# A Mamba and feed-forward layer in float32 on one core: the order of the slots and the shape of the broadcast copies are changed

## The reference

```
x = layernorm(x + mamba(x))
x = layernorm(x + ffn(x))

mamba: x, z   = split(x @ in_proj.T)                    # 512 channels each
       u      = silu(conv4(x) + conv_b)                 # causal, 4 taps, per channel
       dt, B, C = split(u @ x_proj.T)                   # 64, 16, 16
       delta  = softplus(dt @ dt_proj.T + dt_b)         # 512 channels
       h[d,n] = exp(delta[d] * A[d,n]) * h[d,n] + delta[d] * u[d] * B[n]    # over time, 16 states n
       y[d]   = sum_n h[d,n] * C[n] + u[d] * D[d]
       out    = (y * silu(z)) @ out_proj.T
ffn:   silu(x @ w1.T * s1) * (x @ w2.T * s2), two hidden layers of 1024 with gelu, and w3 (256)
```

## Time and profile before

| what | value |
|---|---|
| median of three runs | 3355.04 us |
| the profiled execution | 3354.35 us, of it 3352.5 us from the first to the last instruction |
| mean granted TensorE clock | 0.884 of full speed |
| VectorE busy | 2347.6 us (70%) |
| TensorE matmuls busy | 2793.5 us (83%) |
| ScalarE busy | 2024.4 us (60%) |
| GpSimd busy | 1744.5 us (52%), all in the Mamba stage |
| moved by DMA | 404.11 MB, in 236430 packets |

### The profile page before, as it was taken

The page is one execution under the profiler, slowest core; times in us unless marked ns, Lnnn a source line. Parts: engine busy times, 40 slices in busy tenths (PEclk is TensorE's granted clock), DMA queues, the critical chain, the costliest instruction groups (busy, mean ns, idle before and its releaser), DMA issues. The chain is left out here.

```text
span 3352.5 us, 40081 instructions
## 1 busy us (share of the span) xinstructions
PE 2793.5 (83%) x10946; PEld 1629.1 (49%) x10946; DVE 2347.6 (70%) x2829; ACT 2024.4 (60%) x3344; POOL 1744.5 (52%) x892
## 2 busy tenths in 40 slices
PE   5787887887887878877878875659999999999997
PEld 2232332333333333333323332327888888888886
DVE  1988988989889889888888889444444544444443
ACT  4666666676676676676676666345555555555542
POOL 0878988888888888889788888500000000000000
PEclk8788888878888879888888887769999999999999
DMA  4454545455464554645545454372322221222210
GB/s 138 90 170 126 140 150 145 129 159 130 137 173 105 158 148 120 173 129 135 164 131 139 144 146 125 108 254 93 95 68 88 71 92 63 88 75 88 69 57 14
DMA packets 236430, 404.11 MB, mean 121 GB/s; under 512 B 23120, under 2 KB 61776, under 8 KB 236240
## 3 DMA queue, kind: packets, MB, share of 16 engines
q1 hardware_dynamic: 173328, 292.95, 31.6%
q10 hardware_dynamic: 62912, 109.08, 10.1%
HBM read 278.21 MB, written 123.73 MB: 120 GB/s over the span
## 5 line engine op out<-in xcount | busy, mean ns | idle before, releaser
L964 DVE TENSOR_TENSOR_SCAN h<-bank,state,db 128x512 f32<-128x512 f32 x1024 | 1253.7, 1265 | 64.7 <-ACT bank L700 32.7
L839 POOL TENSOR_TENSOR hc<-h,c_rows 128x1024 f32<-128x1024 f32 x512 | 1199.6, 2370 | 188.6 <-PE bank L482 182.1
L700 ACT ACTIVATE bank<-d_bc,a_neg 128x512 f32<-128x512 f32 x1024 | 694.5, 686 | 427.6 <-DVE h L964 350.2
L1191 PE MATMUL s_bank<-s_end,weights_r 128*128 128x512 f32 x2048 | 472.4, 392 | 23.7 <-DVE s_end L1284 23.7
L948 DVE TENSOR_TENSOR db<-bank,du_bc 128x2048 f32<-128x2048 f32 x192 | 435.6, 2269 | 58.9 <-DMA du_bc<-du_rows 58.8
L1251 ACT ACTIVATE s_h<-s_bank,s_sc 128x512 f32<-128x512 f32 x256 | 176.0, 688 | 486.2 <-PE s_bank L1191 485.9
L1191 PE MATMUL s_bank<-s_mid,weights_r 128*128 128x512 f32 x2048 | 466.8, 389 | 0.0
L1191 PEld LDWEIGHTS s_bank<-s_end,weights_r 128*128 128x128 f32 x2048 | 385.8, 189 | 105.6 <-DVE s_end L1284 26.2
L1191 PEld LDWEIGHTS s_bank<-s_mid,weights_r 128*128 128x128 f32 x2048 | 384.4, 188 | 79.8
L547 PE MATMUL bank<-x_t,w 128*128 128x512 f32 x1088 | 385.1, 486 | 36.2 <-ACT ab L760 29.4
L461 PE MATMUL bank<-bc,w_spread 64*128 64x512 f32 x272 | 152.1, 572 | 279.5 <-DVE db L948 204.4
(11 more groups left out here) (111 smaller groups left out, 3109.5 us busy)
## 6 DMA issues: line engine op xcount, KB each, us to landing
ab<-ab ACTq DMA_DIRECT2D x272, 256.0 KB, 4.0
d_bc<-d_rows SPq DMA_DIRECT2D x256, 256.0 KB, 5.2
du_bc<-du_rows SPq DMA_DIRECT2D x256, 256.0 KB, 8.0
s_abr<-ab SPq DMA_DIRECT2D x128, 512.0 KB, 3.9
w<-w ACTq DMA_DIRECT2D x136, 256.0 KB, 3.7
d_rows<-sp_r SPq DMA_DIRECT2D x64, 256.0 KB, 2.0
du_rows<-sp_w SPq DMA_DIRECT2D x64, 256.0 KB, 2.4
xT_sb<-in_xT SPq DMA_DIRECT2D x16, 512.0 KB, 11.6
```

Source lines behind the costliest of these rows:

```text
L700: act.activation(decays[DECAY_BANK[g]][:], d_bc[c % 2][:, j, :], ACT.Exp, scale=a_neg[:, g:g + 1]).then_inc(decay, 1)
L839: pool.tensor_tensor(hc[:, k % HCSTEPS, at:at + HG], h[:, H_SLOT[k], at:at + HG], c_rows[:, q, :].unsqueeze(1).broadcast_to([P, HG, NT]), ...
L964: dve.tensor_tensor_scan(h[:, H_SLOT[k], j, :], decays[DECAY_BANK[g]][:], db[:, k % DBSTEPS, j, :], state[:, g:g + 1], ALU.mult, ALU.add). ...
L1191: last = pe.matmul(p_h[m % HBANKS][:], weights[:, at:at + P], ins[j][:, k, :], start=k == 0 and j == 0, stop=k == KH - 1 and j == parts - 1)
```

## The change

The change has four parts.

- Slots: the 16 convolution products go into slots 0 to 10 instead of 0 to 15, SiLU of u from slot 17 to 12, x_proj from 18 to 14, the step sizes of quarter 0 from 24 to 20, SiLU of z from 40 to 63, the layer norm's last activations from 11 to 15, the transposes for `ab` from 13 and 17 to 16 and 18, and the `ab` products to a slightly different list, with the waits that go with it.
- TensorE's fold comes right at the start of a slot.
- The store to `x1` stands behind the copies of quarter 3 of the next turn. `x1` has a place for one tile more, which takes the store that the first turn makes with nothing in it. There are 17 stores instead of 16.
- The four copies of a set: before, copy nn fills the 32 partitions of state nn, all four blocks j. Now, copy j fills block j on all 128 partitions, from 32 rows of DRAM that are read four times.

```
-CONV_SLOTS = range(0, KI * TAPS)
+CONV_SLOTS = [2 * i // 3 for i in range(KI * TAPS)]
-SILU_U_SLOT = 17
-XD_SLOTS = range(18, 18 + KI)
-DT_SLOTS = (24, 38, 54, 6)
+SILU_U_SLOT = 12
+XD_SLOTS = range(14, 14 + KI)
+DT_SLOTS = (20, 38, 54, 6)
-SILU_Z_SLOT = 40
+SILU_Z_SLOT = 63
+LN_SLOT = 15
-XT_PLACES = ((13, 2), (17, 1))
-AB_PLACES = ((25, 0), (30, 2), (32, 2), (34, 2), (35, 1), (36, 2), (38, 1), (40, 1), (41, 0), (44, 2), (46, 2),
-             (48, 2), (50, 2), (52, 2), (60, 2), (62, 2))
+XT_PLACES = ((16, 2), (18, 1))
+AB_PLACES = ((23, 0), (25, 0), (28, 2), (30, 2), (32, 2), (34, 2), (36, 2), (38, 1), (40, 1), (41, 0), (44, 2), (46, 2),
+             (48, 2), (50, 2), (52, 2), (60, 2))
...
-        COPIES = 16 * GN
+        COPIES = 16 * JC
...
+            def by_state(rows, j):
+                return rows[j * GD:(j + 1) * GD, :].unsqueeze(0).broadcast_to([GN, GD, NT])
...
-                for nn in range(GN):
-                    sp.dma_start(d_bc[k][nn * GD:(nn + 1) * GD, :, :],
-                                 d_rows[k].rearrange("(j d) t -> d j t", d=GD)).then_inc(d_in[k], 16)
+                for j in range(JC):
+                    sp.dma_start(d_bc[k][:, j, :], by_state(d_rows[k], j)).then_inc(d_in[k], 16)
...
-                for nn in range(GN):
-                    sp.dma_start(du_bc[k][nn * GD:(nn + 1) * GD, :, :],
-                                 du_rows[k].rearrange("(j d) t -> d j t", d=GD)).then_inc(du_in[k], 16)
+                for j in range(JC):
+                    sp.dma_start(du_bc[k][:, j, :], by_state(du_rows[k], j)).then_inc(du_in[k], 16)
...
                 copies(t, 3)
+                store_x1(t)
...
-                sp.wait_ge(ln_out, t.count(SUB, 2 * SUB))
-                sp.sem_inc(waited, 1)
-                sp.dma_start(x1[t.b, rows, :].rearrange("(s p) c -> p s c", p=P), res[:]).then_inc(x1_out, 16)
...
+                    if n % JC == FOLD_AFTER % JC:
+                        now, g = at_group(t, n - FOLD_AFTER)
+                        if exists(now):
+                            fold_step(now, g // JC)
                     if n % JC == 1:
...
-                elif i == 11:
+                elif i == LN_SLOT:
```

More of the change, by code:

```diff
@@ L330, in load_next, with store_x1 @@
                 load_xT(t.following())
+            def store_x1(t):
+                at = (x1[0:TILES].rearrange("(b q) s p c -> b q s p c", q=TILES_B)[t.b, t.tt] if exists(t)
+                      else x1[TILES])
+                sp.wait_ge(ln_out, t.count(SUB, SUB))
+                sp.sem_inc(waited, 1)
+                sp.dma_start(at.rearrange("s p c -> p s c"), res[:]).then_inc(x1_out, 16)
             load_xT(OPENING)
@@ L365, in _ @@
                 tile(t)
-            sp.wait_ge(x1_out, 16 * TILES + 16)
+            store_x1(PAST)
+            sp.wait_ge(x1_out, PAST.count(16, 16))
         @block.tensor
@@ L397, in z_product @@
                         pe.wait_ge(xd_lo, t.count(1, 1))
-                        pe.wait_ge(ab_sb, ab_done(tile_before(t), 1))
+                        pe.wait_ge(ab_sb, ab_done(tile_before(t), 2))
                     else:
@@ L420, in front @@
             def front(t, i):
-                if i in CONV_SLOTS:
-                    conv_product(t, *divmod(i - CONV_SLOTS.start, TAPS))
+                for use, slot in enumerate(CONV_SLOTS):
+                    if i == slot:
+                        conv_product(t, *divmod(use, TAPS))
                 if i in XD_SLOTS:
@@ L444, in step_sizes @@
                 else:
-                    pe.wait_ge(ab_sb, ab_done(tile_before(t), (6, 14, 16)[c - 1]))
+                    pe.wait_ge(ab_sb, ab_done(tile_before(t), (7, 15, 16)[c - 1]))
                 pe.matmul(p_dt[:], w_dt[:, c * P:(c + 1) * P], xd[:], start=True, stop=True).then_inc(dt_mm, 1)
@@ L452, in rows @@
                     pe.wait_ge(z_sb, t.count(KI, 3 + r))
-                    pe.wait_ge(ab_sb, ab_done(tile_before(t), 8 + r))
+                    pe.wait_ge(ab_sb, ab_done(tile_before(t), 9 + r))
                 else:
@@ L492, in project @@
                     elif not exists(nxt):
-                        pe.wait_ge(ab_sb, ab_done(t, 9))
+                        pe.wait_ge(ab_sb, ab_done(t, 10))
                     elif s == 0 and exists(nxt.following()):
@@ L540, in ffn_product @@
                         pe.wait_ge(xd_lo, nxt.count(1, 1))
[L541 to L544, removed]
+                    elif e in (7, 9):
+                        pe.wait_ge(z_sb, nxt.count(KI, 3 if e == 7 else 4))
+                    elif e in (2, 10, 15):
+                        pe.wait_ge(sp_dve, nxt.count(2 * KI, 2 + 2 * (2, 10, 15).index(e)))
                 for k in range(KM):
@@ L579, in tile @@
                             project(t, *part)
[L580 to L583, removed]
                     if exists(t):
@@ L614, in front @@
                         act.activation(z_of(t, j), p_mm[(1 + j) % 2][:], ACT.Copy).then_inc(z_sb, 1)
-                    if i == CONV_SLOTS.start + TAPS * j + TAPS:
+                    if i == CONV_SLOTS[TAPS * j + TAPS - 1] + 1:
                         act.wait_ge(conv_mm, t.count(KI, j + 1))
@@ L939, in _ @@
             dve.sem_inc(y_sb, 1)
-            dve.sem_inc(x1_out, 16)
             def times_b(t, k):
@@ L1727, in program @@
                     a["w1T"], a["w2T"], *rows, w12, x1, ab)
-        x1_rows, out_rows = (v.rearrange("b l c -> (b l) c") for v in (x1, out))
+        x1_rows = x1[1:TILES + 1].rearrange("t s p c -> (t s p) c")
+        out_rows = out.rearrange("b l c -> (b l) c")
         scales = [a["s1"], a["s2"], a["sh1"], a["sh2"]]
@@ L1788 @@
            for k, x in arrays.items()}
-    x1 = nc.dram_tensor("x1", (BATCH, SEQ, DM), F32, kind="Internal").ap()
+    x1 = nc.dram_tensor("x1", (TILES + 1, SUB, P, DM), F32, kind="Internal").ap()
     w12 = nc.dram_tensor("w12", (KH, P, 2, KM, P), F32, kind="Internal").ap()
```

## The result

The changed kernel takes 3942.86 us (median of four runs, 3938.72 to 3945.67) against 3356.94 before (four runs): a ratio of 1.1741, with a 95% interval of 1.1717 to 1.1765. The predicted case, four engines, holds; the point, 4180, was 6% too high, and the time lies in that case's own range, 3845 to 4510.

The account below looks back on a forecast made before the run. VectorE was taken to bound the Mamba stage, at 113 of 128.6 us a tile. Copies confined to four engines add 813 us in 16 tiles and 13 at the opening: 3354 + 813 + 13 = 4180 us, range 3180 to 4510.

Parts of the forecast that it names:

- The predicted case, four engines: Mamba stage's new copies confined to four DMA engines, stalling VectorE: 4180 us, own range 3845 to 4510, chance 0.68.
- The step on engines: DMA: work is dealt out along the outermost dimension, so the new copies' count of four uses four of 16 engines.
- The rate of one engine: DMA: each of the four engines taken at 21 GB/s, between 18.0 and 25.1.
- the same two equations: Mamba tile: pair of copy sets takes L = 27.0 + 29.7 L/T, tile time T = 113 + 4L - 63.2; L 32.4, T 179.4.
- The price of the old shape: DMA: 32-partition copies at 220 to 240 GB/s against 414 for 128-partition loads, a packet costing about twice what it could.
- The slack: Mamba tile: time from first d copy until VectorE would take the du product, 63.2 us over four quarters.
- VectorE's 113 us with no other idle time: Mamba tile: VectorE's work of 113 us plus copy stalls makes the tile time; the order's saving is spent or hidden.
- The order alone: Mamba stage: new slots remove 175 us of VectorE waits, GpSimd takes back 40; worth 135 us, between 0 and 207.
- The opening: Program start: the same pair of copy sets with nothing to cover it, 27 us against 13.3, 13 more.
- Rival A: DMA: copies spread over all 16 engines, du wait of 42 and order's 135 saved; 3177 us, chance 0.22.
- Rival B: Mamba stage: new order only moves stalls, copies cost the same; 3354 give or take 35 us, chance 0.05.
- Rival C: Mamba stage: four engines at best rate, each quarter gains another 2 us as GpSimd's lag shortens; 3700 us, chance 0.05.

Follow-up runs that it names:

- interleaved: Changed kernel with each group's partitions renumbered so the copies' repeat of four stands inside (outermost count 32), still 128 partitions: 3175.02 us, ratio 0.9450 to before.
- shapes: Kernel issuing only copies, seven phases of 16 copies of 256 KB in different shapes: old shape 242 GB/s, eight repeats outermost 141, plain rows 359.
- dt24: Changed kernel with the step sizes of quarter 0 back in slot 24: 4022.52 us, 80 more than the change.
- copies_alone: Kernel before with only the new copies (128 partitions, four repeats outermost), old order kept: 4063.87 us, ratio 1.2095.
- shapes2: Second copies-only kernel, six phases onto 128 partitions, eight or sixteen repeats or blocks outermost, or plain rows: eight blocks of different rows 199 GB/s, plain rows 363.
- order_alone: Changed kernel with the old copies (32 partitions each), everything else of the change kept: 3215.86 us, ratio 0.9572 to before.

## Why the prediction was right, and what was off

- *The step on engines* was right. It was argued from what all transfers of the old trace that fill 16 engines had in common, an outermost count that 16 divides, since no row showed a count of four; shares of 0.26, 0.52 and 0.13 for counts of 4, 8 and 2, and `interleaved`, show it.
- *The rate of one engine* was the mis-sized term: 21 GB/s taken, 23.4 measured (90/(16 x 0.24)) with the row of 1281 us, and 25.3 with nothing beside it. Put into the same two equations, 23.4 gives L = 22.4 + 2 + 26.5 L/T, so L = 29.1 and T = 166.1, and the sum 3967: this one term is 213 of the 237 us between 4180 and 3943. Measured were 27.9 for L as the mean of the tile shown, and 164.8 for T over all tiles. That T comes so close is partly luck: L is still 1.2 too long, 4.8 us a tile, and the idle time put at nothing (below) gives 4.5 back. The quiet stretch of the earlier trace rows, 19.8 GB/s, was a poor witness for an engine kept full of 2 KB packets; why it shows less stays open.
- *The price of the old shape* was too high: "about twice what it could" came from comparing its 220 to 240 GB/s with loads of another packet size. In `shapes`, with the same 2 KB rows, it is 242 against 359, a factor of 1.5. The sum does not use it.
- *The slack* of 63.2 us was right: in the tile shown the pairs take 111.6 us, VectorE waits 47.0 of them, and the rest, 64.6, was covered. By quarters (0, 1, 2, 3) it is 19.8, 15.2, 14.2 and 15.5 where 20.4, 11.4, 14.9 and 16.5 were worked out, so the sum is closer than its parts. Taking quarter 0's move back cost 5.0 us a tile and not 7.1, of it only 3.3 as a longer wait for du (`dt24`).
- *VectorE's 113 us with no other idle time* was nearly right: waits for exponentials (45.7 us) and GpSimd (26.2) stayed, 4.5 us a tile. That the order's saving is hidden in the stalls is only partly so: with the new copies the order is still worth 121 us (`copies_alone` against the change).
- *The order alone* was forecast as 135 us and gave 142, yet for partly other reasons. GpSimd took nothing back (its wait before the scans is 24.7 against 29.9), so the 40 us put down to it were not due. But the waits that were to go, 175 us, went only by 128: the exponentials' wait from 32.7 to 25.4, the one before the softplus step from 67.5 to 12.9, the skip's from 61.5 to 8.2, the low rows' from 13.3 to 0.5. From the first scan to the last the gain is 129 us; another 8 lie behind the last scan, where nothing was forecast. Errors cancelled: that 135 and 142 are so close is luck. That the norm at slot 11 is worth up to 32.7 was wrong too: with SiLU of u at slot 12, leaving it there costs 88.
- *The opening*: the first scan begins at 91.6 us in place of 77.9, 13.7 later; 13 were forecast.
- *Rival A* is what `interleaved` does: 3175, where 3177 was worked out; its terms, 42 and 135, came out as 41 and 142 (against a time before of 3357.6, not 3354). *Rival B* is out, since the order alone gains 4.3%. *Rival C* (3700) overstated both the rate (25.1) and the lag made up, of which nothing shows. The point at which A turns, eight engines, was not tried in this program; phase 3 of `shapes`, 141 GB/s for eight engines with repeats, less than eight times 21, suggests that it would lie higher.
- Of the signs named, the idle time before the product with du (767.8 us in the whole run, some 800 forecast), the DMA share (0.31 in the stage, 0.24 in copies alone) and the unchanged scans and feed-forward stage came as said. The landing time of the du copies could not be read: the profile's page gives none for these copies.

## What to carry to other kernels

Read the outermost dimension of both sides of every transfer before its size: here a broadcast with 2, 4 or 8 repeats outermost gave the whole copy to 2, 4 or 8 engines, and the DMA share in a stretch of these copies alone (0.25 for four) tells it at a glance; beside other traffic it is hidden (0.56). The repeat moved inside, by renumbering partitions in the constant tables, cost nothing in this kernel. A mean DMA share that falls (0.51 to 0.31) while waits for DMA grow was the mark of it. Where slots are written out by hand, take moves apart before crediting them: here the order loses 88 of its 142 us when one move is left out.

## What the hardware showed that was not expected

- Eight engines that all read the same rows of DRAM move 141 to 147 GB/s; eight that read different rows 199. With four (101 and 101) there is no difference.
- Copies of sixteen blocks of eight rows stay at 254 to 271 GB/s, with or without repeats, where 128 plain rows reach 359 to 363 and 32 rows repeated four times inside reach 340. The cause is open.
- Issuing takes SyncE longer the fewer engines share a copy: sixteen copies took 71.0 us to issue with two engines, 33.0 with four, 13.7 to 18.0 with eight and 7.4 to 10.6 with sixteen (`shapes`, `shapes2`). In the changed kernel's tile, four du copies took 9.8 to 15.6 us in place of 1.7 to 2.1.
- ScalarE's own `ab` stores landed later beside the new copies: 5.6 us (median), against 3.1 in `order_alone` and 4.0 before.
